# An attention and expert layer on one core: four steps change places in the slot of a row

## What is computed

```python
x = x + layernorm(attention(layernorm(x)))     # 16 heads of 16 features
x = x + layernorm(ffn(layernorm(x)))           # shared expert + top 1 of 8 routed ones

# attention: ct_q, ct_kv = low-rank projections of x (192 and 64 wide)
q = up_q(ct_q) + rope(wq_r(ct_q));  k = up_k(ct_kv) + rope(wk_r(ct_kv));  v = up_v(ct_kv)
a = softmax(q k^T / 4) v ;  return a wo^T + bo

# ffn: logits = x router_w^T, the best expert per token, its gate by sigmoid
```

## Time and profile before

| | us |
|---|---|
| median of 3 runs | 497.55 (495.1 to 499.42) |
| profiled execution | 496.64 |
| its span | 494.8 |
| TensorE busy in the span | 436.1 (88%) |
| VectorE busy | 252.4 (51%) |
| ScalarE busy | 185.6 (38%) |

### The profile page before, as it was taken

How to read it: one execution, slowest core, us unless ns; L and a number is a source line. 1 busy time by engine, 2 the same in 40 slices (tenths; PEclk the granted TensorE clock), 3 DMA queues, 4 the chain that set the end, 5 groups by cost and what they waited for, 6 DMA issues and landing times.

```text
span 494.8 us, 7794 instructions
## 1 busy us (share of the span) xinstructions
PE 436.1 (88%) x2519; PEld 280.7 (57%) x2520; DVE 252.4 (51%) x591; ACT 185.6 (38%) x383; POOL 134.7 (27%) x195
## 2 busy tenths in 40 slices
PE   3755789999999998989899999999999999999791
PEld 2533456666666664646466565666666666655551
DVE  4243667868686867774867522222222222234665
ACT  1315566666666665545522222222222222221010
POOL 1114141525252515132120011111211110048433
PEclk9977999999999998989999999999999999999897
DMA  8491335363626363601384301111111111123311
GB/s 252 138 93 39 98 77 188 82 198 83 199 73 202 81 190 96 193 1 45 111 275 156 128 23 32 44 42 42 42 45 50 51 44 42 42 86 108 106 42 64
DMA packets 53989, 48.33 MB, mean 98 GB/s; under 512 B 5862, under 2 KB 49638, under 8 KB 53958
## 3 DMA queue, kind: packets, MB, share of 16 engines
q1 hardware_dynamic: 47424, 39.23, 27.3%
q0 software_dynamic: 1872, 5.11, 3.7%
q10 hardware_dynamic: 4662, 3.59, 2.5%
HBM read 25.78 MB, written 9.31 MB: 71 GB/s over the span
## 4 chain that ended last, share of the span: by engine, by line
PE 64%; DVE 15%; POOL 6%; issue 5%; SPq 4%; DMA 3%; ACT 2%; POOLq 0%; ACTq 0%; DVEq 0%
PE bank L1208 42%; PE bank L1212 7%; DVE nmax L946 4%; PE bank L1328 4%; SPq L434 4%; PE bank L1344 3%; PE bank L1292 3%; POOL pv L637 2%; PE bank L1260 2%; PE bank L1268 2%; DMA stacks<-parts_q 2%; DVE wall L976 1%; DVE stats_at L879 1%; POOL rstd_at L535 1%; DVE wall L966 1%
## 5 line engine op out<-in xcount | busy, mean ns | idle before, releaser
L1208 PE MATMUL bank<-wall,stacks 128*128 (+2 forms) x616 | 212.5, 488 | 6.1 <-DVE stacks L1141 5.5
L1208 PEld LDWEIGHTS bank<-wall,stacks 128*128 128x128 f32 x616 | 112.0, 192 | 68.5 <-issue 58.0
L946 DVE TENSOR_REDUCE nmax<-bank 128x2 f32<-128x512 f32 x128 | 85.0, 685 | 52.4 <-PE bank L1292 52.4
L1137 DVE TENSOR_TENSOR stacks<-stacks,bank 128x512 f32<-128x512 f32 x39 | 26.8, 687 | 85.9 <-PE bank L1208 85.9
L1292 PE MATMUL bank<-stacks 96*128 96x256 bf16 x256 | 49.0, 279 | 14.8 <-DMA stacks<-parts_q 8.0
L621 POOL DMA_INDIRECT stacks<-x_sc,row_i x23 | 22.0, 955 | 124.2 <-PE bank L1212 124.2
L821 ACT ACTIVATE stacks<-bank 128x512 f32<-128x512 f32 x39 | 23.3, 597 | 82.5 <-PE bank L1208 82.5
L1344 PE MATMUL bank<-stacks 99*128 99x256 bf16 x256 | 50.3, 280 | 4.4 <-DMA stacks<-mT 2.8
L783 ACT ACTIVATE pv<-bank 128x512 f32<-128x512 f32 x64 | 38.0, 598 | 36.6 <-PE bank L1344 35.7
L1141 DVE COPY stacks<-bank 128x512 f32<-128x512 f32 x39 | 26.9, 690 | 46.4 <-PE bank L1212 46.1
L783 ACT ACTIVATE wall<-bank 128x512 f32<-128x512 f32 x64 | 38.0, 603 | 31.7 <-PE bank L1344 30.8
(11 more groups left out here) (150 smaller groups left out, 513.5 us busy)
## 6 DMA issues: line engine op xcount, KB each, us to landing
wall<-gate_up SPq DMA_DIRECT2D x8, 1024.0 KB, 5.2
stacks<-parts_k SPq DMA_DIRECT2D x96, 64.0 KB, 2.6
stacks<-parts_q SPq DMA_DIRECT2D x91, 64.0 KB, 2.6
wall<-down SPq DMA_DIRECT2D x8, 512.0 KB, 6.2
y_exp<-stacks ACTq DMA_DIRECT2D x23, 128.0 KB, 1.7
x_tok<-wall SPq DMA_DIRECT2D x8, 256.0 KB, 2.6
stacks<-x_tok SPq DMA_DIRECT2D x16, 128.0 KB, 2.3
out<-stacks SPq DMA_DIRECT2D x8, 256.0 KB, 2.2
```

Source lines behind the costliest of these rows:

```text
L946: dve.tensor_reduce(nmax[:, half, qt, 2 * pair:2 * pair + 2], two(sm_bank[u % 2]), AX.X, ALU.max, negate=True).then_inc(sm["sm_max"], 1)
L1137: dve.tensor_tensor(hid, sg, fu[:, :], ALU.mult).then_inc(sm["h_sb"], 1)
L1208: last = pe.matmul(out_ap, lhsT, rhs, start=(n == 0), stop=(n == len(pairs) - 1))
```

## The change

Three tables of steps change by a few places; no instruction is added, taken away or altered. On TensorE `A_QK` moves from head 3 to head 2, right behind `M1`; `E_xn2T` moves from head 2 to head 3, and `E_router` from head 4 to head 5. On VectorE `B_stats` moves from head 5 to head 4 (the copy of the logits stays in head 5), and `B_norm` from head 8, behind `D_div1`, to head 7, ahead of it. On GpSimd `B_power` moves from head 6 to head 5.

```diff
# gpsimd
-            order = {0: ("M1",), 6: ("B_power",), 8: ("A_kres", "M0",),
+            order = {0: ("M1",), 5: ("B_power",), 8: ("A_kres", "M0",),
# vector
-            order = {0: ("E_xn2",), 1: ("A_T",), 5: ("E_router", "B_stats",),
-                     6: ("D_div0",), 8: ("D_div1", "B_norm",), 9: ("N_v",), 11: ("D_y",),
+            order = {0: ("E_xn2",), 1: ("A_T",), 4: ("B_stats",), 5: ("E_router",),
+                     6: ("D_div0",), 7: ("B_norm",), 8: ("D_div1",), 9: ("N_v",), 11: ("D_y",),
# tensor
-            order = {0: ("A_R",), 1: ("A_Q",), 2: ("M1", "E_xn2T",), 3: ("A_QK",), 4: ("E_router",),
+            order = {0: ("A_R",), 1: ("A_Q",), 2: ("M1", "A_QK",), 3: ("E_xn2T",), 5: ("E_router",),
```

## The result

The changed kernel takes 500.99 us (median of 20 runs, 495.81 to 503.4), the kernel before, run beside it, 496.57 us (20 runs, 492.56 to 499.86). The ratio is 1.007, with a 95% interval of 1.0045 to 1.0096. So the change makes the kernel slower, by less than 1% but by more than scatter, and the forecast of 496.2 us missed the sign and the range (493.0 to 499.0). The profiled execution took 500.34 us, its span 498.5, the mean granted clock 0.960 (before 496.64, 494.8 and 0.970).

A forecast was written before the change was run, and what follows sets the result against it. TensorE was taken as the bound in the attention slots, VectorE second. Slot terms -0.24 + 0.47 + 3 x 0.0 - 0.90 - 0.63 gave -1.30 us: 495.3 profiled, 496.2 us median, range 493.0 to 499.0.

The forecast's parts named there:

- part 1: TensorE, paired products ahead of the second norm's turns: 0.27 us gained a slot, not 0.60; the rotation is late next.
- part 2: Router one head later, statistics ahead of it: 0.63 us gained in slots 5 and 6; turns 0.60 us later in slots 2 to 4.
- Slot 1: Statistics between maxima 4 and 5 delay head 7's maxima product 0.96 us; 0.47 us of loss remain, bounds 0.2 and 0.96.
- The 0.24 us of slot 0: Gain in slot 0, where the norm's wait goes but GpSimd's residues end the slot; bounds 0 and 0.3.
- part 3: VectorE, first norm ahead of the second division: its turns come without a wait, giving back 0.33 us in slots 2 to 4.
- my sum: Total over slots 0 to 6: -1.30 us against the profiled execution of 496.64 us, giving 495.3.
- The clock was a rival: Fewer stops in slots 5 and 6 let TensorE's clock hold: a further 1.6 us gone, 494.6 us; chance 0.19.
- Net for slots 2, 3 and 4: 0.0 us each: Gains and delays of the three parts cancel in these slots; bounds -0.15 and +0.2.
- The rival "slower": VectorE, heads 4 to 8 of slots 2 to 4: uncovered statistics stay in the path, costing 2.1 us, 498.3 us; chance 0.15.

The follow-up runs named there:

- with the norm back: Changed kernel with the first norm back behind the second division, other moves kept: 501.63 us, ratio 1.0078; run once more, 500.41 us, ratio 1.0071.
- the early statistics with either place of the rotation: TensorE's moves, VectorE's statistics in head 2 and norm in head 3: 491.32 us; also with rotation in head 0 and second norm in head 1: 487.48 us.
- the early norm with either subtraction: TensorE's moves plus the norm ahead of the second division, statistics not moved: 498.27 us; also with GpSimd's key subtraction on 8 of 256 columns: 494.46 us.
- the two single moves: Kernel before with only the paired products ahead of the second norm's turns: 494.49 us; kernel before with only TensorE's router one head later: 494.3 us.
- the late turns: Changed kernel with the norm back behind the second division, and the first attention-output turns and their division moved to head 7: 493.27 us, ratio 0.9931.
- the fastest kernel: TensorE's moves, statistics in head 2, norm in head 3, with VectorE's rotation in head 0 and second norm in head 1: 487.48 us, ratio 0.9818.

## Why the prediction was wrong

**What held.** The working of TensorE's moves: part 1 with 0.27 us a slot (measured 0.28), with the rotation as what is late next; part 2 with 0.63 us where no statistics stand in between (0.62 in slot 5). Together they were to give slot 5 0.90 us, and with the norm back it went from 24.66 to 23.76. The turns behind the copy of the logits, counted from head 4's scores: 3.42 us forecast, 3.42 measured in slot 3. Slot 1, once the norm had its old duration: 0.47 us forecast, 0.52 measured, with a stop of 0.79 us ahead of a maxima product where I had about 1. And slot 3 with that duration: 25.0 forecast, 25.09 measured. The 0.24 us of slot 0 can't be read, since the start of the program scatters by more.

**The step that failed first: the duration of the norm in part 3.** I took "0.79 for the norm" from its rows in the old place. In the new place the pair takes 1.77. With a margin of 0.07 us for the second division, as the rival said, all of it above that went through: TensorE waited 0.59 us in slot 3 and 1.05 in slot 1, and at full clock slots 3 and 4 came to 25.88 and 25.78 instead of 25.0, slot 1 to 24.55 instead of 23.6. Those four slots, with slot 2 taken at the same 0.8, make 3.4 us over my sum (0.95, 0.8, 0.88, 0.78). In this profile slots 1 to 6 lie 6.3 us over it; the rest is 0.7 us of slot 2's dip and 2.1 us in slots 5 and 6, where the long dip stands. The cause of the duration is shown: with the subtraction cut to 8 columns, and nothing else altered, it is 0.87 and 0.89 us again, in two kernels. The price is 0.94 us a slot where the statistics are not in front (25.59 to 24.65), and in the changed kernel 0.90 us in slot 1 (18.14 to 17.24 from its second quad on) and 0.79 us in slot 3 (25.88 to 25.09), of which 0.38 us come back as a wait for a transfer at the next slot's head.

The Trainium skill ("SBUF — State Buffer", SBUF: two separate sides) says that VectorE and GpSimd share one pair of ports to the on-chip memory as an exclusive lock, held for a whole instruction, and that a VectorE operation with two inputs there takes it against a GpSimd operation that reads there. The norm has two such inputs, rows of x and the broadcast root, and the traces agree: 0.87 us alone, 1.77 and 1.82 beside a subtraction of 1.31 and 1.16. Nothing in the profile before showed the overlap, because the old order never made it; what the profile did show is GpSimd's queue, and I never set it beside the norm's new place. My own count put the norm of slot 4 at 159.28 to 160.1, and the key subtraction stands there at 159.54 to 160.70. I wrote that GpSimd's stream stays the same word for word, which is true, and took it for the same as not being touched.

**The second step: the clock.** I wrote: "In slots 1 to 4 the clock is full with the same stops, so there it can give nothing." But they weren't the same stops: in part 2 I had worked out that the turns come 0.60 us later. The stop for the logits became 1.11 us. In the five traces of kernels whose statistics stand ahead of that copy, with the turns in head 6, slots 2 to 4 hold nine dips in fifteen slots, each beginning 0.2 to 1.0 us behind the start of those turns. In the nine traces without that stop (before, TensorE's moves, the early statistics with either place of the rotation, the early norm with either subtraction, the two single moves, the late turns) they hold none. And taking the stop away with the statistics left in place took away the dips and 7 to 8 us. The clock was a rival in my working only on the side of a gain, and its price of 1.6 us for the dip at the head of slot 6 was too high: with TensorE's moves and no dip there slot 6 takes 21.76 us, 1.23 under before, of which 0.62 are the router's gain if it is that of slot 5. That leaves about 0.6 us for the dip.

**Two separate mistakes, each enough.** With TensorE's moves alone the kernel is at 0.9873. The norm ahead of the division brings it to 1.0024, the statistics ahead of the copy to 1.0078 and 1.0071, both to 1.007. They don't add. The traces say by what: a dip adds 1.9 to 2.3 us to a slot where the norm is in its old place, 0.2 to 0.7 of it by the norm's meeting with GpSimd again, and 0.7 where TensorE would have waited for the second division anyway. Either one by itself uses up all that TensorE's moves gain. My "Net for slots 2, 3 and 4: 0.0 us each" was a sum in which gains of 0.9 us a slot, both real, were given back by moves of VectorE that brought nothing at all. The rival "slower" named the right place, engine and margin (VectorE in heads 4 to 8), with a price of 2.1 us that was too low, as it left out the port and the clock.

**What stays open.** Why a stop of 1.11 us at the copy of the logits is followed by a dip in nine slots and not in the other six, and why one of 1.55 to 1.58 us at the second division (the early norm, four slots) brings none. What else runs around the two differs, and no run here varied one stop's length alone: the statistics ahead of the copy move maxima too, and the late turns change places as well as their wait. That the stop is what brings the dips is the likeliest reading, not shown to the last step. Also the 10.2 us dip of the changed kernel in slots 5 and 6, which made slot 6 24.35 us: a dip of 3.4 to 10.3 us falls in slots 5 and 6 in ten of the fourteen traces here, also in that of the fastest kernel (188 to 198 us), so I don't count it to the change. The four traces without one all have TensorE's moves, as have six of the ten with one; whether the moves make it rarer no run here shows.

## What to carry to other kernels

When a step is moved, its duration moves only if its neighbours do: lay the other engines' streams beside the new place, and where VectorE and GpSimd would both read the on-chip memory there, cost the pair at up to the sum of both. A margin of less than 0.1 us is no margin, and the sum should carry its failure as the likely case. Cost each moved step alone before summing: here TensorE's moves were worth -1.3% and VectorE's took all of it back, while the same two steps of VectorE put where that engine idled were free. And a wait on TensorE can cost more than its length: behind the 1.11 us stop for the logits a stretch of half clock followed in nine slots of fifteen, at 0.7 to 2.3 us each. It is a risk to be priced, not a rule, since the stop of 1.58 us brought none.

## What the runs showed of the hardware

A VectorE operation on 128x256 with two inputs in the on-chip memory and a GpSimd subtraction of 128x512 take turns rather than share: the pair took 1.82 us, against 0.89 beside a subtraction of 0.22 us. Where the norm starts under a running subtraction, it ends 0.68 us after it, early or late (134.41 + 1.16 and 134.43 + 1.82 in one kernel, 136.26 + 1.16 and 136.55 + 1.55 in another). Where the norm starts first, GpSimd waits too: the subtraction grew from 1.16 to 1.31 us in slot 3 of the changed kernel. The clock dips in slots 2 to 4 came as stretches of about 3.4 us at half clock, whatever the slot, and one cost up to 2.3 us of time, more than the 1.7 us that its slower matmuls can lose; the rest, 0.2 to 0.7 us, is TensorE's wait for the norm that the dip pushed onto GpSimd's subtraction. Taking the stop away gave 0.3 to 0.4 us in a slot at full clock, so the dip behind it was several times dearer than the wait itself.
